# Waits put once per engine, PSUM banks released one by one, and new queue orders in a one-core retention and FP4 feed-forward layer

## The reference

```
x = layernorm(x + attn(x));  x = layernorm(x + ffn(x))

attn: q, k = rope(x@Wq), rope(x@Wk)  (8 heads of 16);  v = x@Wv  (8 heads of 32)
      scores = (q k^T / 4) * decay_h^(i-j) for j <= i, else 0;   o = scores @ v
      o = o * rsqrt(mean(o^2) + eps) * g_norm_w;  return (o * silu(x@Wg)) @ Wo
ffn:  quant(a): in blocks of 16: scale = max|a|/6, a/scale rounded to the FP4 grid, times scale
      h = silu(quant(x) @ quant(w_gate)^T) * (quant(x) @ quant(w_up)^T)     (352 wide)
      return quant(h) @ quant(w_down)^T
```

## Time and profile before

| | us |
|---|---|
| median of 3 runs (lowest to highest) | 151.75 (151.49 to 152.52) |
| the profiled execution, its own time | 150.29 |
| its span, first to last instruction | 148.5 |
| busy: PE, DVE | 122.5, 124.4 |
| busy: POOL, ACT | 101.5, 96.3 |
| mean granted TensorE clock | 0.98 |

### The profile page before, as it was taken

One profiled execution on the slowest core, in us unless ns is written; L12 is line 12 of the kernel. 1 busy time (PEld: TensorE's weight loads), 2 busy tenths in 40 slices (PEclk: granted clock), 3 DMA queues, 4 the chain that ended last, 5 costly groups with the idle time before them and its releaser, 6 DMA issues.

```text
span 148.5 us, 3934 instructions
## 1 busy us (share of the span) xinstructions
PE 122.5 (82%) x1206; PEld 75.1 (51%) x1206; DVE 124.4 (84%) x466; ACT 96.3 (65%) x279; POOL 101.5 (68%) x139
## 2 busy tenths in 40 slices
PE   0349487999999999999999999999999886767550
PEld 0123144655466664666667676666674553444340
DVE  0024999978769899999999999999999999999930
ACT  1223724767777877868686869696878666654552
POOL 4012184667868789887888889898989784744552
PEclk9999968999999999999999999999999999999996
DMA  3999950000000000000000000000000000001013
GB/s 119 239 391 380 429 143 4 0 2 4 2 0 4 0 4 2 2 4 0 0 4 0 0 7 2 4 0 0 4 18 10 14 18 18 0 18 34 24 53 93
DMA packets 6407, 7.62 MB, mean 51 GB/s; under 512 B 667, under 2 KB 5531, under 8 KB 6259
## 3 DMA queue, kind: packets, MB, share of 16 engines
q1 hardware_dynamic: 5712, 6.42, 12.8%
q10 hardware_dynamic: 675, 0.94, 2.1%
HBM read 6.31 MB, written 1.05 MB: 50 GB/s over the span
## 4 chain that ended last, share of the span: by engine, by line
PE 70%; DVE 15%; DMA 4%; issue 4%; ACT 2%; POOL 2%; SPq 1%; DVEq 0%; ACTq 0%
PE ps L293 10%; PE ps L317 8%; PE ps L285 6%; PE ps L436 6%; PE ps L415 5%; PE ps L421 5%; PE ps L356 5%; PE ps L383 4%; PE ps L346 4%; DMA tabs<-rope_tables 4%; PE ps L374 3%; PE ps L329 2%; PE ps L428 2%; PE ps L384 2%; PE ps L301 2%
## 5 line engine op out<-in xcount | busy, mean ns | idle before, releaser
L840 POOL TENSOR_TENSOR rstd_h<-ms,minus_half 128x8 f32<-128x8 f32 x16 | 26.3, 1644 | 7.6 <-DVE ms L703 7.6
L851 POOL TENSOR_TENSOR rstd<-veps,minus_half 128x1 f32<-128x1 f32 x32 | 20.2, 641 | 6.6 <-DVE veps L720 6.3
L831 POOL TENSOR_TENSOR qk<-rope_c,rope_s 128x256 f32<-128x256 f32 x16 | 13.1, 819 | 11.9 <-DVE rope_s L677 11.7
L293 PE MATMUL ps<-w_vg,xT 128*128 128x512 f32 x32 | 17.4, 627 | 0.9 <-DVE r L725 0.8
L864 POOL TENSOR_TENSOR hq<-h_grid,hs 128x352 f32<-128x352 f32 x16 | 12.6, 786 | 6.0 <-DVE h_grid L627 6.0
L436 PE MATMUL ps<-wd_T,hT 128*128 128x128 f32 x96 | 14.1, 283 | 2.5 <-ACT hT L464 2.3
L684 DVE TENSOR_TENSOR probs<-ps,causal 128x512 f32<-128x512 f32 x16 | 10.9, 684 | 6.0 <-PE ps L317 6.0
L285 PE MATMUL ps<-w_qk,xT 128*128 128x256 f32 x32 | 12.2, 464 | 4.5 <-DMA w_qk<-in_w_qk 4.5
L436 PEld LDWEIGHTS ps<-wd_T,hT 128*128 128x128 f32 x96 | 12.5, 191 | 4.6 <-ACT hT L464 3.3
L317 PE MATMUL ps<-q_eo,kT 32*128 32x256 f32 x128 | 11.9, 440 | 2.6 <-DVE gate_o L708 2.1
L546 ACT ACTIVATE silu_h<-ps 128x352 f32<-128x352 f32 x16 | 7.4, 464 | 9.8 <-PE ps L415 9.8
(11 more groups left out here) (98 smaller groups left out, 349.3 us busy)
## 6 DMA issues: line engine op xcount, KB each, us to landing
tabs<-rope_tables SPq DMA_DIRECT2D x1, 1536.0 KB, 12.4
out<-x SPq DMA_DIRECT2D x16, 64.0 KB, 1.6
tabs<-rope_tables SPq DMA_DIRECT2D x1, 960.0 KB, 8.5
xT<-x_transposed SPq DMA_DIRECT2D x1, 512.0 KB, 9.6
x_res<-x SPq DMA_DIRECT2D x1, 512.0 KB, 13.5
tabs<-rope_tables SPq DMA_DIRECT2D x1, 384.0 KB, 7.0
wgu_nat<-in_w_gate_up ACTq DMA_DIRECT2D x1, 352.0 KB
xT<-x_transposed SPq DMA_DIRECT2D x1, 320.0 KB, 7.0
```

What stands on the lines that cost most here:

```text
L293: mm(vg_ps, xT[:, c * C:(c + 1) * C], w_vg[:], start=True, stop=True).then_inc(vg_pe, 1)
L831: gp.tensor_tensor(qk[:, c % D, :], rope_c[:, c % D, :], rope_s[:, c % D, :], ALU.add).then_inc(qk_p, 1)
L840: gp.tensor_tensor(rstd_h[:, c, :], ms[:, c, :], minus_half[:], ALU.pow).then_inc(rms_p, 1)
L851: gp.tensor_tensor(rstd[n][:, c, :], veps[n][:, c, :], minus_half[:, 0:1], ALU.pow).then_inc(ln_p[n], 1)
```

## The change

There are six edits.

1. Each engine's waits go through `FirstWaits`, which remembers the highest count that this engine has already waited for on each semaphore, and puts a wait only if it asks for more.
2. PE remembers which tile lies in each PSUM bank, and a step that writes a bank waits for the reader of that tile alone. Where that reader's result is the step's own input, there is no wait for the bank. `scores` frees its banks one by one, between its matmuls.
3. `copy_v` and `silu_of_g` become one step with one signal, `vg_act`, at the end of the silu; `rope_cos` and `rope_sin` become one step, `rotate`.
4. The weights' quantisation on DVE is cut into six steps, which are spread over other stages: `weights_amax(0)` comes in the first stage, ahead of the first `rotate`; `weights_inv(0)`, `weights_ratio(0)`, `weights_amax(1)` and `weights_inv(1)` ahead of the first `mask_scores`.
5. `transpose_weights` becomes two steps, which stand in PE's stages 2 and 3 (before: 0 and 1).
6. The loops of PE, ACT, DVE and POOL have new orders and offsets, and run from stage -5 to 31 (before: -4 to 27).

```diff
+class FirstWaits:
+    def __init__(self, engine):
+        self.engine = engine
+        self.seen = Counter()
+    def wait_ge(self, semaphore, count):
+        if self.seen[semaphore] < count:
+            self.engine.wait_ge(semaphore, count)
+            self.seen[semaphore] = count
...
-            def after_vg_and_att():
-                if filled["vg"]:
-                    pe.wait_ge(sg_act, filled["vg"])
-                    pe.wait_ge(v_act, filled["vg"])
-                if filled["att"]:
-                    pe.wait_ge(ln_v[0]["sum"], filled["att"])
+            def free_vg_bank():
+                if tile.get(5) == "vg":
+                    pe.wait_ge(vg_act, filled["vg"])
+                elif tile.get(5) == "att":
+                    pe.wait_ge(ln_v[0]["sum"], filled["att"])
...
             def scores(c):
                 pe.wait_ge(qkT_act, 3 * (c + 1))
-                after_scores(0)
-                after_scores(2)
-                if filled["oT"]:
-                    pe.wait_ge(oT_act, filled["oT"])
-                if filled["tr"]:
-                    pe.wait_ge(gate_v, filled["tr"])
-                if filled["yT"]:
-                    pe.wait_ge(yT_act, filled["yT"])
                 for j in range(NP):
+                    free_scores_bank(j)
...
             def up(c):
-                pe.wait_ge(xqT_act, c + 1)
-                after_up_down_and_state()
+                pe.wait_ge(wT_act, 2)
+                free_up_bank()
+                pe.wait_ge(xqT_act, c + 1)
...
-            def copy_v(c):
+            def copy_v_and_silu(c):
                 act.wait_ge(vg_pe, c + 1)
-                copy(v_sb[:, c % D, :], vg_ps[:, 0:VD]).then_inc(v_act, 1)
-            def silu_of_g(c):
-                act.wait_ge(vg_pe, c + 1)
-                nc.scalar.activation(silu_g[:, c % D, :], vg_ps[:, VD:2 * VD], ACT.Silu).then_inc(sg_act, 1)
+                copy(v_sb[:, c % D, :], vg_ps[:, 0:VD])
+                nc.scalar.activation(silu_g[:, c % D, :], vg_ps[:, VD:2 * VD], ACT.Silu).then_inc(vg_act, 1)
```

More of the change, by code:

```diff
@@ L437, in down @@
                 last.then_inc(down_pe, 1)
[L438 removed]
+                fill(7, "down")
             for s in range(FIRST, LAST):
                 run = stage_runner(s)
[L442 to L450 removed]
@@ L451, in _ @@
[L451 to L460 removed]
+                run(gate, -4)
+                run(state_product, 0)
+                if s == 3:
+                    transpose_down_weights()
+                run(from_state, 0)
@@ new lines, in _ @@
+                run(transpose_y, -1)
+                run(values, 0)
+                run(up, -4)
+                run(out_projection, -1)
+                run(transpose_o, 0)
+                run(transpose_h, -7)
+                run(transpose_qk, 1)
+                if s == 2:
+                    transpose_gate_up_weights()
+                run(project_vg, 1)
+                run(transpose_xq, -3)
+                run(down, -7)
+                run(scores, 1)
+                run(project_qk, 2)
```

428 lines of the change are left out of this document (213 added, 215 removed).

## The result

The changed kernel takes 154.39 us (153.42 to 155.06, four runs); before, run beside it, takes 152.12 us (151.49 to 152.52, four runs). The ratio is 1.015, 95% interval 1.008 to 1.022: slower by 1.5%, and not by noise. The forecast was 147.1. Some executions of these kernels run 1.5% or more over the fastest of their kernel; the ratios and intervals in this document leave those out, the medians don't.

What follows compares the result with a forecast made beforehand. DVE was taken as the limit from 13 to 33 us and in the drain, PE in the steady stage. Terms -3.9 + 0.35 - 1.2 - 0.9 + 0.95 = -4.7 us from 151.75 gave 147.1; range 144.5 to 151.9, forecast's own 144.5 to 149.5.

Steps and rivals of the forecast that it cites:

- The new order in the steady stage: PE's and DVE's steps in one full stage: all waits met at 6.94 us, four by only 0.15 to 0.2; no cost.
- the bad end: Full stages: an allowance of up to 0.5 us a stage in case the new order's waits are not met.
- The weights in the first idle time: DVE's start: weights' quantisation moved into its wait for the first scores; gain 3.9 us, bounds 2.0 and 4.2.
- The delay of the first product: DVE's start: weights_amax(0) ahead of the first rotate makes the first scores 0 to 0.8 us later; 0.35 taken.
- Waits put once, banks one by one: PE's full stages: 0.11 us less in each of eleven; gain 1.2 us, bounds 0 and 2.5.
- DVE's mask later: DVE's drain: 2.0 us less work left behind the last mask; gain 0.9 us, bounds 0 and 2.0.
- the end: Last output norms and DMAs: ten norms behind the last copy_hT instead of seven; loss 0.95 us, bounds 0.4 and 1.5.
- the slower rival: Steady stage: x_amax waits for ln1_norm, delaying h_product and project_vg by 0.7 us a stage; 154.8 us, one in ten.
- the second (DVE's start isn't what counts): First chunks: held by their own chain, not DVE's work, so the weights and mask terms go; 151.9 us, 13 in a hundred.
- The third (waits cost PE nothing): PE ahead of scores: the hole is the switch to small matmuls and ACT's signal, and stays; 148.3 us, one in ten.
- The fourth: More than the sum: PE's slow clock from 13 to 33 us goes (1.3 us), drain gains 1.1 more; 144.7, seven in a hundred.
- the merged signals: Readers of v also wait for the silu of g, about 0.3 us; taken as no cost in full stages.

Runs made afterwards that it cites:

- e7: The changed kernel with a few places swapped in POOL's and DVE's queues so that colliding instructions no longer overlap: 150.0 us, 0.990 of the kernel before.
- e2: The changed kernel with POOL's rotate_add and h_value writing constants instead of reading their inputs: 147.5 us, 0.977 of the kernel before.
- e11: The changed kernel with the mended orders of e7, PE's state_product right ahead of values and DVE's next_state behind the next stage's x_grid: 149.5 us, 0.987.
- e14: e11 with DVE's next_state one place earlier, ahead of x_grid: 149.5 us, 0.990 of the kernel before.
- e4: The kernel before with only waits put once, banks released one by one and merged signals, in the old orders: 150.1 us, 0.988.
- e8: e4 with DVE's weights steps moved forward together with their partners, such as ACT's weights_magic(0): 147.8 us, 0.973 of the kernel before.
- e5: The kernel before with only DVE's weights steps moved: first reduction behind the first product, four steps ahead of the first mask: 152.3 us, 1.004.
- e15: e14 with weights_amax(0) behind the first rotate and ln2_norm 12 stages behind instead of 16: 148.7 us, 0.983 of the kernel before.
- e13: e7 with ACT's ln2_norm 12 stages behind instead of 16: 149.7 us, 0.988 of the kernel before.
- e10: A separate copying kernel of DVE and POOL instruction pairs started together, with a short DVE reduction ahead; two-operand DVE instruction beside POOL's sum: 1.04 us.

## Why the prediction was wrong

**The step that failed** is "The new order in the steady stage", and in it: "All waits are met at 6.94 us ... I take no cost for them". The layout used DVE's durations from the trace of before, where hardly any DVE instruction with SBUF operands alone lay across a reading POOL one. It laid out PE and DVE, and left out what each POOL instruction would lie beside. The new orders put `h_ratio` under `rotate_add` and `x_scale` under `h_value`, 0.86 us more in DVE's stage. DVE's own work, 7.60 - 0.86 = 6.74 us, would have fitted the 6.94. The stage is 0.66 us over the forecast, and e7 takes back 0.53 of it by order alone, with the same computation. In time this term was put at 0 and is 4.4 us (after against e7; 3.7 by their ratios, and e2 as the upper end). The prediction kept "up to 0.5 us a stage for the bad end", but these are in neither its sum nor its range: eleven such stages would be 5.5 us, and its upper end for the forecast was 149.5. Its own sign of being wrong, full stages of over 7.1 us, came true, and PE waits at the first of the places that it named there, `project_vg`.

The trace of before had one sign of this. `h_scale` on the same shape took 0.32 us at 64.92, under POOL's select of 64.58 to 65.22, and 0.20 in the next stages; in the changed kernel it takes 0.16. The same DVE instruction with two durations asks for a look at POOL.

**A second part of the same step:** "there are six changes between the kinds in a stage, before and after". In the new order there are seven, since `state_product` stands between `gate` and `from_state` and not beside `values`. With the collisions gone the stage is 7.07, not 6.94, and the slot of `state_product` costs 0.11 us more (0.25 against 0.14), near the 0.09 that the prediction read for one change. That removing it gives 6.94 wasn't shown (e11, e14). A third: the prediction had `q_even` ahead of `scores` as tight in the full stages, but didn't look at the stages in which `down` hasn't begun. From the fifth to the eighth scores nothing covers ACT's `q_even` there. In e7 these scores are 6.56 to 6.69 us apart, in e4 5.94. Of the 0.75 us of the stage from 43.78, 0.30 lie between `transpose_xq` and the scores (0.50 against 0.20), 0.10 in the scores before, 0.22 around `project_vg` and 0.11 at `state_product`. PE's weight load waits for `q_even` up to 0.8 us (37 to 57 us):

```profile
PEld ps L329 <- ACT q_eo L482: 1.8, 3, 0.8
```

**The weights in the first idle time: nearly twice too large.** From the first to the fourth scores the changed kernel gains 3.79 us, where 3.9 stood, with the clock at 1.00. That match is luck in part: 0.75 of it is the transposes of the down weights, which only moved. From the fourth to the ninth it loses 3.79, of which the table above and e7 (32.98 us there) put 0.95 on collisions. Another 0.86 is those transposes and 0.76 the first `down`, both moved into this stretch; the rest is what the new order leaves uncovered, as above. In the orders of before the term is worth 2.0 us at the fourth scores and 2.2 in time (e8 against e4), at the lower of its bounds and with the clock's share in it, and nothing if ACT's step stays where it was (e5). Its condition, that the partners move as well, wasn't stated.

**The delay of the first product: mis-sized.** 0.35 us was the forecast, 2.15 came in this execution. Of these the tables' own landing is 1.2 (8.9 us against 7.7), which the change doesn't touch; the reduction is the other 0.9, as in the other six executions that have it ahead (0.9 to 1.0). The count of bytes gave the landing of the weights at 6.5 to 7.3 us; the reduction started at 8.69. Bytes moved by a queue are not the landing of the tile. And in all seven the weights land 0.1 to 0.3 us ahead of the tables, early or late together with them, so of the reduction's 1.2 us all but that comes on top. The late tables are also most of what two of the signs are off by: the first mask came at 15.26, not 13.4, and the scores of chunk 1 at 19.22, not 17.3.

**Waits put once, banks one by one: right.** 7.05 to 6.94 us a stage, shown by e4; the time gained 1.9 us (1.1 to 2.7) where 1.2 stood. By the rule that the prediction weighed against it (the Trainium skill, page "VectorE: DVE Perf Modes", section "The DRAIN you can't avoid") this term would have been nothing; that page speaks of VectorE, and e4 shows a gain on PE, though not how much of it is the waits and how much the banks. The old gap ahead of the scores went too, though in the changed kernel `down` filled it.

**DVE's mask later, and the end.** The end is right: from the last norm's end to the span's end it is 3.05 us in the changed kernel and in e14, and 1.9 with `ln2_norm` at -12 (e15); e7 and e13 have 2.9 and 2.1. That is 0.8 to 1.1 us for 0.95. What the later mask gave isn't shown. From the last scores to the end the changed kernel still takes 1.6 us less than before, where the sum had about 0. The waits alone give 0.4 of that (e4 takes 35.64 us there). The rest, with the later norms' 0.8 to 1.1 added, is some 2 us that the new orders gained in the drain. The later mask is one part of it, and that one `down` less is left behind the last scores may be another. No run separates them.

**The rivals.** The time is near that of the slower rival (154.8), which is in part luck, since that sum held gains that didn't come. Its place is right: PE waits at `project_vg` for `ln1_sum`, and the loss of 0.66 us a stage lies above its 0.56. Its mechanism isn't what happened: DVE didn't wait for `ln1_norm` ahead of `x_amax`; two of its own instructions took longer. A bound of 0.5 us a stage on the forecast's bad end was too low for either, and 0.10 too small a chance where the slack was 0.15 to 0.2 us. Of the others, the second (DVE's start isn't what counts) is contradicted by the 2.0 us of e8, though it is what e5 measured, where only DVE's steps moved. The third (waits cost PE nothing) is refuted by e4. The fourth had the slow stretch of the clock go, and it went, from 0.91 to 1.00 between 13 and 33 us; its 1.3 us beside the first term can't be told apart.

**Left open:** whether the new orders can reach 6.94, what the later mask alone is worth, how the gain of e4 divides between waits and banks, what the clock gives of e8's 2.0 us, and whether the merged signals cost anything.

## What to carry to other kernels

When a queue is re-ordered, lay out DVE beside POOL as well as beside PE: for each DVE instruction with SBUF operands alone, ask which reading POOL instruction it lies across, and put the PSUM readers and reductions there instead. A duration from the trace of before holds only beside the neighbours it had. Work moved into an idle time can be held up by the next wait in front of the critical step (e5), so move its partners on the other engines with it; and a term that is right in the first stages must be followed until the stage repeats.

## What the runs showed of the hardware

- A DVE instruction of 128x352 with two SBUF operands takes 1.04 us if a POOL sum of 128x256 has begun some 60 ns before it, and 0.70 beside a select that has begun 70 ns before it, against 0.515 alone; started first, it makes the sum take 1.06 us for 0.73 (e10).
- POOL's power reads two SBUF tiles and lasts 1.64 us, and yet DVE's instruction beside it takes 519 ns; if DVE is first, the power takes 1.98 (e10).
- A scale of 128x8 on DVE takes 0.69 us, not 0.16, if the sum has begun 70 ns before it, and ends some 40 ns behind it; it grows to 0.25 us even beside a fill, which reads nothing (e10).
- The same loads land up to 1.8 us earlier or later from one profiled execution to the next: the first product's tables, issued at 1.7 us each time, took between 5.8 us (e2, e13) and 7.6 us (e14) to land.
